# One matmul of 65 columns for two of 33 in a linear attention kernel, with new orders on every engine

## The chip, the core and the metric

The kernel runs on one NeuronCore of a Trainium2 chip. Five engines work side by side and meet at semaphores only: TensorE (PE in the views), VectorE (DVE), ScalarE (ACT), GpSimd (POOL) and SyncE (SP), which here issues DMAs. Each takes its instructions in the order in which the program gives them. The metric is the device time of one execution in microseconds, lower is better.

## The reference, cut to what matters

```
x = x + 0.5 * ffn_block(layernorm(x))
x = x + linear_attention(layernorm(x), Wq, Wk, Wv, Wo, bo)
x = x + 0.5 * ffn_block(layernorm(x))

# linear_attention, B=2, L=4096, E=512, 16 heads of 32
phi_q = elu(q) + 1 ;  phi_k = elu(k) + 1
S = S + phi_k[:, None] * v[None, :]         # running 32x32 state of each head
z = z + phi_k
out = (phi_q @ S) / (sum(phi_q * z) + eps)
```

The feed-forward block chooses `cap = s_len // n_head` tokens for each of its 16 heads; with 2 as the first size of x that is 0, so nothing is added and each block is a normalisation with `ln_g` and `ln_b`. These stages are the first and the last of the kernel.

## The kernel before

The 4096 positions are cut into 32 chunks of 128, and both batch elements (b = 0, 1) are worked in each. Inside a chunk the attention is done densely: scores of 128 x 128 per head, masked causally, times the values, plus the product of the queries with the state left by the earlier chunks. To keep fp32 accuracy with fp16 operands every number is held as a high and a low fp16 half, and a product is made of three matmuls: high with high, high with low, low with high (`PASSES`).

One pass of the loop works on four chunks at once, each at another stage: the newest is loaded and normalised (`front_...`), the next is projected to k, q and v (`project_k`, `project_q`, `project_v`), the next goes through attention (`scores`, `attend`, `update`, `project_out`), and the oldest is normalised a last time and stored (`back_...`, `store_y`). `ops(st)` gives the pieces of one pass. The function `body` of each engine writes the order of its pieces out by hand; `opening` and `closing` do so for the first and last chunks. Between them `body` runs 29 times. Nothing else sets an order: a piece waits by semaphores for its inputs and for the buffers that it overwrites, and all that stands behind it on its engine waits with it.

The attention of one chunk on the engines:

- TensorE, `scores(b, hg)`: 4 heads into one PSUM bank, `SC`. VectorE masks half of them (`mask`), ScalarE copies the other half (`copy_scores`) and GpSimd masks those (`cut`). ScalarE makes the high half of the masked scores `A` (`split_a`), GpSimd the low half.
- TensorE, `attend(b, hf)`: 8 heads, 4 matmuls each: `QS` with the state `SS` (L1640), then the three of `PASSES`, `A` with `VN` (L1643). All have 33 columns: 32 values and a column for the denominator (`DA`). The sums lie in the two banks of `AV`.
- ScalarE, `sums(b)` (L776) copies the 16 denominators to `DEN`. VectorE inverts them (`reciprocals`, L1205) and `quotient(b)` (L1216) multiplies `AV` by them into `TP`. ScalarE and VectorE split `TP` into halves of `ATTN` (`attn_half`, L784, `attn_low`, L1235). SyncE turns it by a DMA (`turn_attn`), and `project_out(b)` (L1675) reads the result `AT`.
- TensorE, `update(b, hf)` (L1661) writes this chunk's share of the state into `AV`, once `quotient` has read it. VectorE adds it to `S` (`add_s`, L1228), and `attend` of the other b may then overwrite `AV`.

The projections share the banks `PJ`: `project_q(b)`, `project_v(b)`, `project_out(b)`, `project_k(b)` follow each other in `PJ[b]`. So `project_v(b)` waits for `low_q(b)` (L1174), the last reader of q, and `project_out(b)` for `low_v(b)` (L1195), the last reader of v. `project_k(b)` waits for the turned `XT` (`turn_x`), `scores(b, 0)` for the turned `KS` and `QS` (`turn_k`, `turn_q`). `front_stats` and `back_gain` (L1273), `back_y` (L1282) are pieces of the first and the last stage on VectorE.

Of the kernel before, what the change touches and what calls it, by code (L numbers as in the profile page):

```python
# [8 lines left out]
P = 128  # L9
BATCH, LEN, E = 2, 4096, 512  # L10
# [3 lines left out]
C = 128  # L14
# [30 lines left out]
WIDTH = H // 2 * DA  # L45

# [15 lines left out]
def build(nc, x, Wq, Wk, Wv, Wo, attn_bo, ln_g, ln_b, out):  # L62
    with ExitStack() as ctx:
# [9 lines left out]
        def sig(name, per, by=1, base=0):  # L73
# [14 lines left out]
        sumsq = sb("sumsq", [P, 4, GROUPS])  # L88
# [34 lines left out]
        VN = [sb(f"VN{p}", [P, BATCH, 2, H, DA], F16) for p in range(2)]  # L123
# [17 lines left out]
        wsq = Y[:, 0]  # L141
# [5 lines left out]
        AV2 = ps("AV", (P, 2, E))  # L147

# [49 lines left out]
                                                     sig("rden_done", 2), sig("attn_done", 2))  # L198
        st_filled = sig("st_filled", 4)
# [66 lines left out]
        def _(sp):  # L266
# [79 lines left out]
            def opening():  # L346
                early, first, second = ops(Step(0, -2)), ops(Step(0, -1)), ops(Step(0, 0))
                early.turn_x(0)
                early.turn_x(1)
                first.turn_k(0)  # L350
                first.turn_k(1)
                first.turn_q(0)
                first.turn_x(0)
                first.turn_x(1)
                first.turn_q(1)
                second.turn_k(0)
# [4 lines left out]
            def closing():  # L361
                fourth, third, second = ops(Step(0, steps - 3)), ops(Step(0, steps - 2)), ops(Step(0, steps - 1))
                fourth.turn_q(0)
                fourth.turn_attn(0)
                fourth.turn_attn(1)
                fourth.turn_x(0)
                fourth.turn_x(1)
                fourth.turn_q(1)
# [12 lines left out]
            sp.wait_ge(y_stored.sem, y_stored.at(steps - 1, 1))  # L381
# [3 lines left out]
        def _(pool):  # L385
# [131 lines left out]
            def body(st):  # L517
# [5 lines left out]
                prev.split_a(1, 3)  # L523
                prev.spread_q(1)
                prev.rstd1_of_x1()
                now.cut(0, 1)
                prev.spread_k(1)
                now.rstd0_of_x()
                now.split_a(0, 0)
                now.split_a(0, 1)  # L530
                now.split_a(0, 2)
                now.x1_bias()
                now.cut(0, 3)
                now.rstd2_of_x2()
                prev.split_s(0)
                now.split_a(0, 3)
                now.cut(1, 1)
                now.split_a(1, 0)
                now.spread_k(0)
                prev.split_s(1)  # L540

            def opening():
# [6 lines left out]
                first.spread_k(1)  # L549
                first.rstd1_of_x1()  # L550
                first.spread_q(0)
                first.spread_q(1)
                second.x1_bias()
# [5 lines left out]
                second.split_a(0, 2)  # L559
                second.split_a(0, 3)  # L560
                second.cut(1, 1)
# [6 lines left out]
            def closing():  # L568
                fourth, third, second, last = ops(Step(0, steps - 3)), ops(Step(0, steps - 2)), ops(Step(0, steps - 1)), ops(Step(0, steps))
                fourth.cut(1, 3)  # L570
                fourth.spread_q(0)
                fourth.split_a(1, 1)
                fourth.split_a(1, 2)
                fourth.split_a(1, 3)
                fourth.rstd1_of_x1()
                fourth.spread_k(1)
                third.cut(0, 1)
                third.split_a(0, 0)
                fourth.spread_q(1)
                third.cut(0, 3)  # L580
                fourth.split_s(0)
                fourth.split_s(1)
                third.rstd2_of_x2()
                third.split_a(0, 1)
                third.split_a(0, 2)
                third.split_a(0, 3)
                third.spread_k(0)
                third.spread_k(1)
                third.spread_q(0)
                third.cut(1, 1)  # L590
                third.split_a(1, 0)
                third.split_a(1, 1)
                third.cut(1, 3)
                third.spread_q(1)
                third.split_a(1, 2)
                third.split_a(1, 3)
                second.split_a(0, 0)
                second.split_a(0, 2)
                third.split_s(0)
                third.split_s(1)  # L600
                third.x1_bias()
                second.rstd2_of_x2()
                second.split_a(1, 0)
                second.split_a(1, 2)
# [7 lines left out]
        def _(act):  # L612
            a = nc.scalar


            def square(j, c):

                m = W_ORDER[j]
                act.wait_ge(w_loaded[m], 16)
                if j or c:  # L620
                    act.wait_ge(w_summed, j * GROUPS + c)
                a.activation(wsq, wnat[m][:, c], ACT.Square, accum_out=sumsq[:, m, c:c + 1]).then_inc(w_summed, 1)  # L622
# [8 lines left out]
            def ops(st):  # L631
# [3 lines left out]
                class Ops:  # L635
# [8 lines left out]
                    def store_y():  # L644
# [4 lines left out]
                        a.dma_start(out[:, bass.ds(back * C, C), :].rearrange("b p e -> p b e"), Y[:]).then_inc(y_stored.sem, 16)  # L649

# [108 lines left out]
                    def v_half(b):  # L759
# [6 lines left out]
                        a.activation(VN[st.parity(1)][:, b, HI, :, 0:D], PJ[b].rearrange("p (h d) -> p h d", h=H),  # L766
                                     ACT.Copy, scale=V_SCALE).then_inc(v_hi.sem, 1)

                    def sums(b):
# [5 lines left out]
                        av = AV2[:, :, 0:2 * QUADS * DA].rearrange("p f (h d) -> p f h d", d=DA)  # L775
                        a.activation(DEN[:, b], av[:, :, :, D], ACT.Identity, bias=den_eps[:, 0:1]).then_inc(den_done.sem, 1)  # L776
# [19 lines left out]
            def body(st):  # L796
                now, prev = ops(st), ops(st.before())
                prev.copy_scores(1, 3)
                prev.back_scale(1)
                prev.sums(0)  # L800
                prev.q_half(0)
# [1036 lines left out]
```

## Time and profile before

| what | value |
|---|---|
| median of 3 runs | 933.3 us (933.2 to 936.84) |
| the profiled execution | 931.69 us |
| its span, first to last instruction | 929.8 us |
| TensorE busy | 900.6 us, 97% |
| VectorE busy | 832.3 us, 90% |
| ScalarE busy | 756.8 us, 81% |
| GpSimd busy | 705.3 us, 76% |
| mean granted TensorE clock | 0.996 |

The profiled execution's time holds 1.89 us outside its span, and lies 1.6 us under the median. Busy times are unions of the engines' own instructions. A view in order of time gives for each row its start, the duration, and in square brackets how long the engine had been idle before it and what released it. The duration of a matmul reaches past the start of the next one, since they are pipelined: the distance between starts is what a matmul costs, and the same holds, to a smaller degree, for the other engines.

### The profile page before, as it was taken

Reading aid. Unit: us, or ns where it says so; the run is one execution under the profiler, and the core shown is the slowest. Engines: PE = TensorE matmul, PEld = TensorE weight load, DVE = VectorE, ACT = ScalarE, POOL = GpSimd, SP = SyncE. Lnnn points to the kernel's source line nnn. Section 1 sums busy time; section 2 is a strip of 40 time slices with the busy share of each in tenths; the row PEclk is TensorE's granted clock in tenths of the full one; section 3 lists DMA queues with packets and bytes.
Section 4 is the critical chain, followed back from the end, with each engine's and each line's share of the span. In section 5 each row is a group of like instructions: output and inputs, shape, how many; then the busy total and the mean of one; then the engine's idle time right before and its main releaser. Section 6 shows DMA issues by size and latency. Waiting matters only on the chain.

```text
span 929.8 us, 30016 instructions
## 1 busy us (share of the span) xinstructions
PE 900.6 (97%) x10278; PEld 527.0 (57%) x10278; DVE 832.3 (90%) x1539; ACT 756.8 (81%) x1323; POOL 705.3 (76%) x869
## 2 busy tenths in 40 slices
PE   4999999999999999999999999999999999999995
PEld 3455555655555665555565655556555556555562
DVE  6989898999999999999999999999999999988885
ACT  6988888888888888888888888888888888888752
POOL 1469777779777778877778977777887777897661
PEclk9999999999999999999999999999999999999999
DMA  8576698876677767668767667776766876766873
GB/s 292 94 152 133 141 179 160 150 138 151 147 162 159 162 138 150 151 143 180 158 146 143 148 147 160 159 165 137 154 147 144 176 158 150 142 129 125 155 121 69
DMA packets 421421, 139.82 MB, mean 150 GB/s; under 512 B 402560, under 2 KB 402560, under 8 KB 421376
## 3 DMA queue, kind: packets, MB, share of 16 engines
q1 hardware_dynamic: 404496, 106.73, 61.6%
q10 hardware_dynamic: 16880, 32.51, 10.6%
q8 instruction: 26, 0.43, 0.2%
q14 instruction: 19, 0.16, 0.1%
HBM read 21.76 MB, written 16.78 MB: 41 GB/s over the span
## 4 chain that ended last, share of the span: by engine, by line
PE 85%; DVE 5%; DMA 4%; ACT 2%; issue 2%; POOL 1%; SPq 0%; ACTq 0%; POOLq 0%; DVEq 0%
PE PJ L1564 48%; PE PJ L1675 17%; PE AV L1643 8%; PE SC L1616 6%; PE AV L1661 5%; PE AV L1640 2%; DMA AT<-ATTN 2%; DMA A<-in_L_attn_Wk_dram 1%; DMA KS<-KN 1%; ACT Y L622 1%; DVE TP L1273 1%; DVE AM L1151 1%; DVE wT L1065 0%; DVE Y L1282 0%; ACT QN L722 0%
## 5 line engine op out<-in xcount | busy, mean ns | idle before, releaser
L1564 PE MATMUL PJ<-wT,XT 128*128 128x512 f16 x2304 | 524.8, 380 | 1.4 <-DMA XT<-XH 0.6
L1564 PEld LDWEIGHTS PJ<-wT,XT 128*128 128x128 f16 x2304 | 216.9, 98 | 245.4 <-issue 3.9
L490 POOL TENSOR_TENSOR A<-AM,A 128x512 f16<-128x512 f32 x252 | 288.2, 1164 | 32.1 <-ACT A L757 32.1
L1675 PE MATMUL PJ<-wT,AT 128*128 128x512 f16 x768 | 176.1, 379 | 2.7 <-DMA AT<-ATTN 2.6
L480 POOL TENSOR_SCALAR_AFFINE_SELECT AM<-AM 128x512 f32<-128x512 f32 x124 | 79.6, 642 | 113.1 <-ACT AM L744 113.1
L757 ACT ACTIVATE A<-AM 128x512 f16<-128x512 f32 x256 | 154.0, 631 | 12.3 <-POOL AM L480 8.9
L1675 PEld LDWEIGHTS PJ<-wT,AT 128*128 128x128 f16 x768 | 71.1, 97 | 80.1 <-DMA AT<-ATTN 4.1
L1643 PE MATMUL AV<-VN,A 128*128 128x33 f16 x3072 | 116.2, 178 | 0.0
L1640 PE MATMUL AV<-SS,QS 128*128 128x33 f16 x1024 | 111.6, 178 | 1.2 <-DVE TP L1216 1.2
L1643 PEld LDWEIGHTS AV<-VN,A 128*128 128x128 f16 x3072 | 108.8, 96 | 3.5
L1151 DVE TENSOR_TENSOR AM<-SC,causal 128x512 f32<-128x512 f32 x132 | 89.7, 682 | 18.2 <-PE SC L1616 18.2
L1640 PEld LDWEIGHTS AV<-SS,QS 128*128 128x128 f16 x1024 | 98.1, 96 | 5.3 <-POOL A L490 1.7
L744 ACT ACTIVATE AM<-SC 128x512 f32<-128x512 f32 x124 | 74.4, 600 | 23.5 <-PE SC L1616 23.4
L1616 PEld LDWEIGHTS SC<-QS,KS 96*128 96x128 f16 x1024 | 68.1, 97 | 32.2 <-issue 0.9
L1616 PE MATMUL SC<-QS,KS 96*128 96x128 f16 x1024 | 83.7, 219 | 1.5 <-DVE AM L1151 0.6
L702 ACT ACTIVATE PHI<-PJ,inv_scale 128x512 f32<-128x512 f32 x64 | 43.6, 682 | 41.9 <-PE PJ L1564 41.9
L513 POOL TENSOR_TENSOR SS<-S,SC_HI 128x528 f16<-128x528 f32 x62 | 73.7, 1189 | 3.3 <-ACT SC_HI L792 3.3
L423 POOL TENSOR_TENSOR X1BO<-X,obias 128x1024 f32<-128x1024 f32 x32 | 75.5, 2360 | 0.2 <-DVE X L1246 0.2
L498 POOL COPY KN<-KN 128x1024 f16<-128x1024 f16 x64 | 66.4, 1037 | 8.4 <-ACT KN L732 8.4
L722 ACT ACTIVATE QN<-PJ,f_scale 128x1024 f16<-128x1024 f32 x64 | 72.0, 1127 | 0.2
L1111 DVE SCALAR_TENSOR_TENSOR X<-TP,stat,shift 128x512 f32<-128x512 f32 x64 | 47.7, 747 | 19.4 <-POOL X1BO L423 19.2
L776 ACT ACTIVATE DEN<-AV,den_eps 128x16 f32<-128x16 f32 x64 | 17.9, 279 | 57.5 <-PE AV L1643 57.5
(106 smaller groups left out, 1574.9 us busy)
## 6 DMA issues: line engine op xcount, KB each, us to landing
out_dram<-Y ACTq DMA_DIRECT2D x31, 512.0 KB, 3.2
X<-in_L_attn_x_dram ACTq DMA_DIRECT2D x30, 512.0 KB, 3.5
X<-in_L_attn_x_dram SPq DMA_DIRECT2D x2, 512.0 KB, 8.0
A<-in_L_attn_Wk_dram SPq DMA_DIRECT2D x1, 1024.0 KB, 8.0
A<-in_L_attn_Wq_dram SPq DMA_DIRECT2D x1, 1024.0 KB, 10.2
QS<-in_L_attn_Wv_dram SPq DMA_DIRECT2D x1, 1024.0 KB, 12.4
QS<-in_L_attn_Wo_dram SPq DMA_DIRECT2D x1, 1024.0 KB, 15.9
XT<-XH SPq DMA_TRANSPOSE x64, 3.5
```

The costliest lines, as they stand in the source:

```text
L423: g.tensor_tensor(X1BO[:, st.parity(1)], X1[:], obias[:].unsqueeze(1).to_broadcast([P, BATCH, E]), ALU.add).then_inc(x1bo_done.sem, 1)
L480: g.affine_select(out=am, in_=am, compare_op=ALU.is_ge, fill=0.0, base=0, pattern=[[0, QUADS], [1, C]], channel_multiplier=-1).then_inc(sc ...
L490: g.tensor_tensor(A[:, b, LO, hg], AM[:, k % 4], A[:, b, HI, hg], ALU.subtract).then_inc(a_lo.sem, 1)
L513: g.tensor_tensor(SS[:, b], S[:, b], SC_HI[:, b], ALU.subtract).then_inc(s_lo.sem, 1)
L744: a.activation(AM[:, k % 4], SC[hg % 2][:], ACT.Copy, scale=SUM_DOWN).then_inc(sc_copied.sem, 1)
L757: a.activation(A[:, b, HI, hg], AM[:, k % 4], ACT.Copy).then_inc(a_hi.sem, 1)
L1151: v.tensor_tensor(AM[:, k % 4].rearrange("p (h q) -> p h q", h=QUADS), SC[hg % 2][:].rearrange("p (h q) -> p h q", h=QUADS), causal[:].uns ...
L1564: ins = t_.matmul(PJ[b], XT[:, w, c, b * C:(b + 1) * C], wT[m_][:, m, c, :], start=(c, w, m) == todo[0], stop=(c, w, m) == todo[-1])
L1616: ins = t_.matmul(SC[hg % 2][:, h * C:(h + 1) * C], KS[cur][0:STACK, head, b * C:(b + 1) * C], QS[cur][0:STACK, head, b * C:(b + 1) * C], ...
L1640: t_.matmul(to, QS[cur][:, head, b * C:(b + 1) * C], SS[:, b, hf, j * DA:(j + 1) * DA], start=True, stop=False)
L1643: ins = t_.matmul(to, A[:, b, w, hg, h * C:(h + 1) * C], VN[cur][:, b, m, head, :], start=False, stop=(w, m) == PASSES[-1])
L1675: ins = t_.matmul(PJ[b], AT[:, b, w, c * C:(c + 1) * C], wT[3][:, m, c, :], start=(c, w, m) == todo[0], stop=(c, w, m) == todo[-1])
```

## The change

In `attend`, the high half of `A` meets high and low values in one matmul: `VN` now holds for each head 32 high values, the denominator's column and 32 low values side by side (`DV` = 65 columns). The product of `A` high with the low values therefore lands beside the rest, in columns of its own. It has to be added later: ScalarE copies these columns of `AV` to `VL` (`spare_sums`), and VectorE adds them to the others into `TP` (`join_sums`). The 8th head of a bank has no room for 65 columns (7 x 65 + 33 = 488 of 512), so it is done as before, and `VL` is zero there. `quotient` then multiplies `TP` in place. `update` waits for `join_sums` instead of `quotient`, and `DEN`. Its matmuls of low values have 32 columns instead of 33.

All orders written out by hand are new. In the opening the four squares of each weight matrix are one instruction, an Exp on one column stands ahead of all else on ScalarE, and TensorE takes the norms of the third matrix ahead of the first projection. In the closing the last tile is scaled, finished and stored in two halves of 256 columns. A bound in the scale of q and k goes from 64 to 32, which changes values and no instruction.

```diff
+DV = DA + D
+WIDE = H // 2 - 1
-        VN = [sb(f"VN{p}", [P, BATCH, 2, H, DA], F16) for p in range(2)]
+        VN = [sb(f"VN{p}", [P, BATCH, H, DV], F16) for p in range(2)]
+        VL = sb("VL", [P, 2, H // 2, D])
+        def heads_of_av(first, last, to):
+            return bass.AP(AV2, first, [[2 * E, P], [E, 2], [DV, to], [1, last - first]])
...
+                    def spare_sums(b):
+                        act.wait_ge(*av_filled.upto(s, 2 * b + 1))
...
+                        a.activation(VL[:, :, 0:WIDE], heads_of_av(DA, DV, WIDE), ACT.Copy).then_inc(low_copied.sem, 1)
...
+                    def join_sums(b):
+                        dve.wait_ge(*low_copied.upto(s, b))
+                        dve.wait_ge(*den_done.upto(s, b))
...
+                        v.tensor_tensor(TP[b][:].rearrange("p (f h d) -> p f h d", f=2, d=D), heads_of_av(0, D, H // 2),
+                                        VL[:], ALU.add).then_inc(av_summed.sem, 1)
...
-                            t_.matmul(to, QS[cur][:, head, b * C:(b + 1) * C], SS[:, b, hf, j * DA:(j + 1) * DA],
-                                      start=True, stop=False)
-                            for w, m in PASSES:
-                                ins = t_.matmul(to, A[:, b, w, hg, h * C:(h + 1) * C], VN[cur][:, b, m, head, :],
-                                                start=False, stop=(w, m) == PASSES[-1])
+                            if j < WIDE:
+                                t_.matmul(AV2[:, hf, j * DV:(j + 1) * DV], a_high, vn, start=True, stop=False)
+                            else:
+                                t_.matmul(to, a_high, vn[:, 0:DA], start=True, stop=False)
+                                t_.matmul(AV2[:, hf, j * DV:j * DV + D], a_high, vn[:, DA:DV], start=False, stop=False)
+                            t_.matmul(to, a_low, vn[:, 0:DA], start=False, stop=False)
+                            ins = t_.matmul(to, QS[cur][:, head, b * C:(b + 1) * C], SS[:, b, hf, j * DA:(j + 1) * DA],
+                                            start=False, stop=True)
...
                     def update(b, hf):
-                        pe.wait_ge(*attn_done.upto(s, b))
+                        pe.wait_ge(*av_summed.upto(s, b))
+                        pe.wait_ge(*den_done.upto(s, b))
...
             # TensorE, body
-                prev.project_v(1)
                 now.scores(0, 0)
                 now.scores(0, 1)
+                prev.project_v(1)
+                now.scores(0, 2)
+                prev.update(1, 0)
+                now.scores(0, 3)
                 prev.project_out(0)
-                now.scores(0, 2)
-                now.scores(0, 3)
-                prev.update(1, 0)
                 prev.update(1, 1)
```

VectorE, in the loop, from `add_s(0)` to `attn_low(1)`, before (names with their buffer numbers; `S<-AV` is `add_s`, `QN<-PJ` `low_q`, `TP<-AV,RDEN` `quotient`):

```order
L1228 SCALAR_TENSOR_TENSOR S<-AV,S 128x528
L1235 SCALAR_TENSOR_TENSOR ATTN<-TP0,ATTN 128x512
L1273 SCALAR_TENSOR_TENSOR TP1<-X2,stat2,TP1 128x512
L1174 SCALAR_TENSOR_TENSOR QN<-PJ,f_scale,QN 128x16x32
L1282 SCALAR_TENSOR_TENSOR Y<-TP1,stat2,shift 128x512
L1205 RECIPROCAL RDEN<-DEN 128x16
L1216 TENSOR_TENSOR TP1<-AV,RDEN 128x512
L1195 SCALAR_TENSOR_TENSOR VN0<-PJ,VN0 128x16x32
L1235 SCALAR_TENSOR_TENSOR ATTN<-TP1,ATTN 128x512
```

and now, with `TP1<-AV,VL` being `join_sums(1)`:

```order
L1267 SCALAR_TENSOR_TENSOR S<-AV,S 128x528
L1110 BN_STATS raw<-X 128x6
L1197 SCALAR_TENSOR_TENSOR PJ<-PHI,PJ 128x512
L1312 SCALAR_TENSOR_TENSOR TP1<-X2,stat2,TP1 128x512
L1274 SCALAR_TENSOR_TENSOR ATTN<-TP0,ATTN 128x512
L1334 SCALAR_TENSOR_TENSOR Y<-TP1,stat2,shift 128x512
L1204 SCALAR_TENSOR_TENSOR QN<-PJ,f_scale,QN 128x16x32
L1235 RECIPROCAL RDEN<-DEN 128x16
L1246 TENSOR_TENSOR TP1<-AV,VL 128x512
L1255 TENSOR_TENSOR TP1<-TP1,RDEN 128x512
L1181 TENSOR_TENSOR AM<-SC0,causal 128x512
L1274 SCALAR_TENSOR_TENSOR ATTN<-TP1,ATTN 128x512
```

`low_q(1)` was the 4th from `add_s(0)` and is the 7th; `low_v(0)` stood ahead of `attn_low(1)` and comes behind it.

TensorE, in the loop, from the last heads of `attend(1, 1)`, before:

```order
L1640 MATMUL AV<-SS,QS 128x33
L1643 MATMUL AV<-VN,A 128x33 x3
L1564 MATMUL PJ<-wT,XT 128x512 x12
L1616 MATMUL SC<-QS,KS 128x128 x8
L1675 MATMUL PJ<-wT,AT 128x512 x12
L1616 MATMUL SC<-QS,KS 128x128 x8
L1661 MATMUL AV<-VN,KN 128x33 x32
```

and now (the 8 heads of `update(1, 0)` follow the last row shown, 2 matmuls each):

```order
L1708 MATMUL AV<-VN,A 128x33
L1709 MATMUL AV<-VN,A 128x32
L1710 MATMUL AV<-VN,A 128x33
L1711 MATMUL AV<-SS,QS 128x33
L1678 MATMUL SC<-QS,KS 128x128 x8
L1626 MATMUL PJ<-wT,XT 128x512 x12
L1678 MATMUL SC<-QS,KS 128x128 x4
L1730 MATMUL AV<-VN,KN 128x33
```

The first two `scores` moved ahead of `project_v(1)`, and `update(1, 0)` ahead of `project_out(0)`.

ScalarE, in the loop, from `sums(1)` to `attn_half(1)`, before:

```order
L776 ACTIVATE DEN<-AV,den_eps 128x16
L766 ACTIVATE VN<-PJ 128x16x32
L683 ACTIVATE TP<-X,offset,rstd 128x512
L784 ACTIVATE ATTN<-TP 128x512
L732 ACTIVATE KN<-PHI,f_scale 128x16x32
```

and now:

```order
L755 ACTIVATE KN<-PHI,f_scale 128x16x32
L799 ACTIVATE DEN<-AV,den_eps 128x16
L809 ACTIVATE VL<-AV 128x2x224
L661 DMA out_dram<-Y 128x2x512
L767 ACTIVATE AM<-SC 128x512
L789 ACTIVATE VN<-PJ 128x16x32
L817 ACTIVATE ATTN<-TP 128x512
```

`spare_sums(1)` (`VL<-AV`) stands behind `sums(1)`, and the store of the finished chunk, which stood behind `copy_scores(0, 3)`, behind it.

## Rows read from the trace of the kernel before

**Rows 1.** Busy time by stretch: window, length, each engine (instructions), clock, DMA
```profile
0.00:30.00 30.00, 15.46 (x66) 10.12 (x67) 22.32 (x64) 21.49 (x47) 6.95 (x22) 1.00 0.76 237
30.00:60.00 30.00, 28.26 (x222) 15.99 (x221) 27.40 (x55) 27.80 (x50) 15.97 (x20) 1.00 0.57 123
...
360.00:420.00 60.00, 60.00 (x747) 35.82 (x744) 55.51 (x104) 51.15 (x90) 49.56 (x60) 1.00 0.68 146
...
900.00:929.80 29.80, 18.91 (x205) 9.92 (x202) 18.83 (x33) 7.32 (x13) 8.19 (x10) 0.94 0.25 54
```

**Rows 2.** TensorE in order of time, one chunk: start, duration, line, operation, count
```profile
415.44 0.39 PE L1616 MATMUL SC<-QS,KS 96*128 96x128 f16 x4
...
416.49 2.75 PE L1564 MATMUL PJ<-wT,XT 128*128 128x512 f16 x12
419.08 0.97 PE L1661 MATMUL AV<-VN,KN 128*128 128x33 f16 x32
419.89 2.75 PE L1564 MATMUL PJ<-wT,XT 128*128 128x512 f16 x12
422.48 0.18 PE L1640 MATMUL AV<-SS,QS 128*128 128x33 f16 x1
...
424.11 2.75 PE L1564 MATMUL PJ<-wT,XT 128*128 128x512 f16 x12
426.70 0.61 PE L1616 MATMUL SC<-QS,KS 96*128 96x128 f16 x8
427.14 2.75 PE L1675 MATMUL PJ<-wT,AT 128*128 128x512 f16 x12
...
442.85 0.38 PE L1616 MATMUL SC<-QS,KS 96*128 96x128 f16 x4
```

**Rows 3.** VectorE in order of time, same chunk
```profile
421.24 0.70 DVE L1228 SCALAR_TENSOR_TENSOR S<-AV,S 128x528 f32<-128x528 f32 x1
...
422.45 0.75 DVE L1273 SCALAR_TENSOR_TENSOR TP<-X,stat,TP 128x512 f32<-128x512 f32 x1
423.11 0.75 DVE L1174 SCALAR_TENSOR_TENSOR QN<-PJ,f_scale,QN 128x512 f16<-128x512 f32 x1
...
424.97 0.70 DVE L1216 TENSOR_TENSOR TP<-AV,RDEN 128x512 f32<-128x512 f32 x1
425.58 0.68 DVE L1195 SCALAR_TENSOR_TENSOR VN<-PJ,VN 128x512 f16<-128x512 f32 x1
426.36 0.69 DVE L1235 SCALAR_TENSOR_TENSOR ATTN<-TP,ATTN 128x512 f16<-128x512 f32 x1
```

**Rows 4.** ScalarE in order of time, same chunk
```profile
424.38 0.27 ACT L776 ACTIVATE DEN<-AV,den_eps 128x16 f32<-128x16 f32 x1 [1.74 <-PE AV L1643]
424.55 0.59 ACT L766 ACTIVATE VN<-PJ 128x512 f16<-128x512 f32 x1
...
425.74 0.59 ACT L784 ACTIVATE ATTN<-TP 128x512 f16<-128x512 f32 x1
...
427.78 0.61 ACT L744 ACTIVATE AM<-SC 128x512 f32<-128x512 f32 x1
```

**Rows 5.** VectorE in the first chunks, two operations that TensorE waits for
```profile
40.02 0.75 DVE L1174 SCALAR_TENSOR_TENSOR QN<-PJ,f_scale,QN 128x512 f16<-128x512 f32 x1 [0.24 <-ACT QN L722]
...
53.06 0.68 DVE L1181 SCALAR_TENSOR_TENSOR PHI<-PHI,PJ 128x512 f32<-128x512 f32 x1
```

**Rows 6.** TensorE in the first chunks, the two matmul groups that waited
```profile
40.91 2.75 PE L1564 MATMUL PJ<-wT,XT 128*128 128x512 f16 x12 [0.36 <-DVE QN L1174]
...
53.80 2.76 PE L1564 MATMUL PJ<-wT,XT 128*128 128x512 f16 x12 [0.15 <-DVE PHI L1181]
```

**Rows 7.** DMA issues of 431 to 433 us: kind, count, us to landing
```profile
XT<-XH SPq DMA_TRANSPOSE x1, 3.6
```

**Rows 8.** DMA issues of 184.1 to 186.1 us, an early chunk
```profile
XT<-XH SPq DMA_TRANSPOSE x1, 4.4
```

**Rows 9.** DMA issues of 427 to 428 us
```profile
AT<-ATTN SPq DMA_TRANSPOSE x1, 3.1
```

More of the change, by code:

```diff
@@ L536, in body @@
                 now.split_a(0, 3)
+                prev.split_s(1)
                 now.cut(1, 1)
+                now.spread_k(0)
                 now.split_a(1, 0)
-                now.spread_k(0)
-                prev.split_s(1)
             def opening():
@@ L548, in opening @@
                 first.spread_k(0)
-                first.spread_k(1)
                 first.rstd1_of_x1()
                 first.spread_q(0)
+                first.spread_k(1)
+                second.x1_bias()
                 first.spread_q(1)
-                second.x1_bias()
                 second.rstd0_of_x()
@@ L973, in closing @@
                 second.split_a(1, 1)
+                second.split_a(1, 2)
                 third.s_half(1)
@@ L976, in closing @@
                 second.back_scale(0)
-                second.split_a(1, 2)
+                second.back_scale(1)
+                second.spare_sums(0)
                 second.split_a(1, 3)
-                second.back_scale(1)
+                second.sums(1)
                 second.attn_half(0)
-                second.sums(1)
+                second.spare_sums(1)
                 second.attn_half(1)
@@ L1297, in body @@
-                prev.phi_q(1)
-                prev.add_s(0)
-                prev.attn_low(0)
-                prev.back_gain(1)
-                prev.low_q(1)
-                prev.back_y(1)
-                prev.reciprocals(1)
-                prev.quotient(1)
-                prev.low_v(0)
-                prev.attn_low(1)
+                prev.phi_q(1)
+                prev.back_gain(1)
+                prev.attn_low(0)
+                prev.back_y(1)
+                prev.low_q(1)
+                prev.reciprocals(1)
@@ L1307, in body @@
+                prev.join_sums(1)
+                prev.quotient(1)
+                now.mask(0, 0)
+                prev.attn_low(1)
+                prev.low_v(0)
+                now.front_stats(1)
+                now.mask(0, 2)
+                prev.x_low(0)
+                prev.low_v(1)
                 prev.low_k(1)
-                now.mask(0, 0)
-                prev.x_low(0)
+                prev.add_out(0)
+                prev.x_low(1)
                 now.front_mean(0)
                 now.front_mean(1)
-                prev.low_v(1)
@@ L1358, in opening @@
                 top_norm(1)
+                scale_w(1)
                 w_low(0, 1)
                 w_low(0, 2)
-                scale_w(1)
                 early.x_low(0)
+                early.x_low(1)
                 w_low(0, 3)
@@ L1521, in closing @@
                 last.back_y(0)
-                last.back_gain(1)
-                last.back_y(1)
+                last.back_gain_part(0)
+                last.back_gain_part(1)
+                last.back_y_part(0)
+                last.back_y_part(1)
             closing()
@@ L1746, in opening @@
                 second.scores(1, 0)
+                second.scores(1, 1)
                 second.project_q(0)
-                second.scores(1, 1)
                 second.scores(1, 2)
@@ L1788, in closing @@
                 second.scores(0, 1)
+                third.attend(1, 0)
                 second.scores(0, 2)
-                third.attend(1, 0)
                 third.attend(1, 1)
@@ L1794, in closing @@
                 second.scores(1, 0)
+                third.update(1, 0)
                 second.scores(1, 1)
-                third.update(1, 0)
                 third.update(1, 1)
+                second.scores(1, 2)
                 third.project_out(0)
                 third.project_out(1)
-                second.scores(1, 2)
                 second.scores(1, 3)
```

445 lines of the change are left out of this document (240 added, 205 removed).

## The prediction

> **What bounds the kernel now.** I read the busy time by stretch first. In the middle TensorE is busy 60.00 of 60 us, VectorE 55.51, ScalarE 51.15, GpSimd 49.56; TensorE is idle only in the first 60 us (14.54 + 1.74) and in the last 30 (10.89) [rows 1]. Then one chunk in order of time: from 415.44 to 442.85 no row of TensorE names a wait, so a chunk costs 27.41 us, all of it matmuls [rows 2]. The loop has 29 chunks, 795 of 929.8 us. VectorE has only some 2.1 us of a chunk left (4.49 of 60).
>
> **What the wide matmul gives.** From 422.48 to 424.11 stand the 64 matmuls of `attend(1, 0)` and `(1, 1)`, so 33 columns cost 25.5 ns. Eight of 128 columns cost 0.44 us (426.70 to 427.14), 55 ns each, and twelve of 512 cost 2.59 (416.49 to 419.08), 216 ns [rows 2]. 65 columns stand in no row. They can't cost less than 33 (25.5), and if they cost twice that (51) nothing is won. The line through 55 and 216 gives 0.419 ns a column and 28.6 ns at 65; I take it, since the larger shapes lie on it and only the smallest sits on a floor. An `attend` of 8 heads then takes 7 x (28.6 + 51) + 4 x 25.5 = 659 ns against 815, so a chunk's four save 0.62 us (0.71 at 25.5, 0 at 51). If TensorE stayed the bound: 0.62 x 32 chunks = 20 us.
>
> The Trainium skill, "TensorE: Matmul & The Clock Gate", Part 1, has start to start as columns over 2.4 GHz plus 2.5 ns, with a floor of some 25 ns. By that 65 columns are 29.6 ns, and a chunk would save 0.59 instead of 0.62. It speaks against the idea that half of the matmul's columns come free, and the rows agree with its floor (25.5).
>
> **What the change adds.** Per chunk VectorE gets two `join_sums`, of the form of `quotient` [rows 3]: 0.70 long, 0.61 from start to start when other work follows, 1.22 a chunk. Its 25.3 become 26.5, and its spare time in a chunk of 26.8 would be 0.3. ScalarE gets two copies of 448 values a partition; 16 values take 0.27, 512 take 0.61 [rows 4], so 0.56 each. ScalarE has 4 us left in a chunk, that is covered unless TensorE waits for it. So the question is who waits at the new places. I laid one chunk of the new order out by hand, each operation at the distances of rows 3 and 4 (0.60 or 0.61 for most on VectorE, 0.66 where `back_gain` stands, 422.45 to 423.11). Handoffs: matmul to ScalarE 0.27 (424.11 [rows 2] to 424.38 [rows 4]); ScalarE to VectorE 0.03 (425.74 + 0.59 to 426.36); VectorE to TensorE 0.14 and 0.06 (40.02 + 0.75 to 40.91; 53.06 + 0.68 to 53.80 [rows 5, 6]), I take 0.10. A dependent operation of VectorE starts some 0.04 after the end of its source, an estimate by the ScalarE handoff.
>
> **First new wait, `project_v(1)` for `low_q(1)`.** TensorE reaches it after `update(0, 1)` in 2.59 (`project_v(0)`) + 1.32 (two `attend`) + 0.44 (two `scores`) = 4.35 us. VectorE can begin `add_s(0)` only when that update is done, and now has seven operations up to `low_q(1)`, where it had four and had started them with others behind: 0.27 + `add_s` 0.61 + `front_stats` 0.60 + `phi_q` 0.61 + `back_gain` 0.66 + `attn_low` 0.60 + `back_y` 0.66 + `low_q` 0.75 + 0.10 = 4.86. `project_v(1)` starts 0.51 late in each chunk. In the kernel before `low_q(1)` ended at 423.86 and `project_v(1)` began at 424.11: it was already close.
>
> **Second new wait, `project_out(0)` for `low_v(0)`.** From the end of `attend(1, 1)` TensorE needs 0.44 + 2.59 + 0.22 + 0.41 + 0.22 = 3.88 us of its own (two `scores`, `project_v(1)`, `scores`, `update`, `scores`). The chain beside it: 0.27, `sums` 0.17 (424.38 to 424.55), `spare_sums` 0.56, 0.03, `join_sums` 0.70 + 0.04, `quotient` 0.70, 0.03, `attn_half` 0.59, 0.03, `attn_low` 0.60, `low_v` 0.68, 0.10: 4.50 [rows 3, 4]. So `project_out(0)` starts 0.62 late in all; the first wait is contained in that. Before, `low_v(0)` stood ahead of `attn_low(1)` and there was no `join_sums`, so it hung on none of this.
>
> A chunk is then 27.41 - 0.62 + 0.62 = 27.41: the matmuls' gain is waited away at the same place in every chunk. Uncertainties: 0.04 either way from the handoff, 0.10 less at 25.5 ns for 65 columns, 0.15 more if ScalarE or VectorE is still at another operation when its turn comes.
>
> **Other moved steps, with one answer.** `update(0, 0)` waits for `join_sums(0)`: the copy is ready about 1.9 us into the chunk, the sum at 2.7, TensorE comes at 3.46 (0.22 + 0.66 + 2.59). Cover 0.7, given by `project_q(1)`. `scores(0, 0)` moved 2.6 us ahead and needs `QS`, of which the DMA lands near 8.2 by my layout, when TensorE arrives; what it waits, up to 0.5, is part of the wait at `project_v(1)`. GpSimd (`split_s`, `x1_bias`, `spread_k` moved) is needed by nobody at once: the layout leaves over 0.6 everywhere.
>
> **DMA.** `project_k(1)` waits for `XT`. Before, `x_low(1)` ended some 4.65 us ahead of it. Now, counted from the start of `low_v(0)`: seven operations on VectorE lead to the end of `x_low(1)` at 5.03, its DMA is issued 0.10 later and lands 3.6 later [rows 7], at 8.73; TensorE arrives at 0.68 + 0.10 + 2.59 + 0.41 + 2.59 + 2.59 = 8.96. The slack shrinks to 0.23. In early chunks (100 to 200 us) the same DMA takes 4.4 [rows 8], which makes it 0.57 late; four such chunks: +2.3. `project_out(1)` for `AT` (3.1 [rows 9]) keeps 0.5.
>
> **Ends.** Opening: merged squares free ScalarE some 1.1 us for each of the first two weights, but TensorE now waits for the third matrix's norm ahead of the first projection. Idle there is 16.28 in all, most of it weights not yet loaded; I take -0.5 (-2.5 to +1.5). Closing: two chunks without a first stage, where VectorE has air, give 2 x -0.62; the last chunk's chain gets longer by the copy and the sum twice (+0.9 on the one that ends last) less its faster matmuls (-0.3), and the halves of the last tile save 0.3: -0.9 (-3 to +2).
>
> **Sum.** 29 chunks x 0.0, +2.3, -0.5, -0.9 = +0.9 on the profiled span of 929.8, 930.7, or 932.6 with the 1.89 around it. That execution lies 1.6 under the median of 933.3, so against the median 934.2.
>
> **Rivals.** (1) *TensorE stays the bound.* If VectorE's operations stand closer than my layout, the waits vanish, a chunk is 26.8, and the time 934.2 - 18 = 916. For it: 2.1 us idle on VectorE against 1.2 added. Against: it needs two chains to shrink by 0.5 and 0.6. Chance 0.14. (2) *Part of the gain.* Some 0.25 to 0.4 of each 0.6 is recovered, as one operation fewer in the way (0.3 on average) would do: 0.3 x 29 = 9, so 925. Chance 0.20. (3) *The DMA decides, slower.* Above 3.83 us for `XT` in the loop TensorE waits at `project_k(1)` too. It is late by 0.37 if the transposes take 4.2 instead of 3.6: 0.37 x 29 = 11, so 945. For it: 4.4 is on record; against: the store of 512 KB moved away from this transpose. Chance 0.17. (4) *The wide matmul costs two narrow ones.* Then 0.62 comes back on the second chain: 934.2 + 18 = 952. Nothing in the rows suggests it; 0.03.
>
> **How the numbers follow.** The forecast, both waits and an unchanged chunk, has 0.46; its own range is 928 to 941 (29 x -0.1 to +0.15, and the ends). The range given reaches from 919, which leaves out rival 1, to 946, which leaves out rival 4 and a tail of rival 3: 0.19 in all. A measurement tells 0.5% (4.7 us) from no change: faster takes rivals 1 and 2 and 0.03 of the forecast, 0.37; slower rivals 3 and 4 and 0.04 of it, 0.24; same 0.39.
>
> **What would show it.** In the middle TensorE should be idle some 0.6 us a chunk, in two waits, at `project_v(1)` for `QN` and at `project_out(0)` for `VN`, and two starts of the same piece 27.4 apart. An `attend` of 8 heads should take 0.66, `spare_sums` 0.56, `join_sums` 0.70. VectorE should be over 96% busy. If TensorE shows 60.00 again, rival 1 is right; if it waits for the DMA of `XT`, rival 3; if 65 columns cost 51 ns, rival 4. The prediction falls if VectorE finds `add_s(0)` ready with work already done ahead, or if its operations stand less than 0.6 apart.

## The result and the profile after

The changed kernel takes 969.1 us (median of 6 runs, 967.0 to 971.8) against 933.5 (6 runs): ratio 1.037, 95% interval 1.036 to 1.039. The forecast was 934.2 with a range of 919 to 946: the time lies outside it, on the side that had a chance of 0.24. The profiled execution has a span of 966.9, 37.1 more than before.

From the page of the changed kernel, the busy time, the chain that ended last, and the group of `project_out` (busy, mean ns | idle before, and what ended it):

```profile
span 966.9 us, 28559 instructions
...
PE 901.4 (93%) x9382; PEld 513.6 (53%) x9382; DVE 870.9 (90%) x1600; ACT 789.6 (82%) x1365; POOL 708.8 (73%) x869
...
PE 48%; SPq 13%; DMA 11%; DVE 8%; issue 4%; ACT 0%; DVEq 0%; POOL 0%; ACTq 0%
...
L1744 PE MATMUL PJ<-wT,AT 128*128 128x512 f16 x768 | 176.3, 379 | 29.2 <-DMA AT<-ATTN 26.4
```

Only 48% of the chain is TensorE (85% before); 13% is SyncE's queue issuing transposes and 11% their flight. `project_out` (L1744) waited 26.4 us for `AT`, a DMA for which it waited 2.6 us before, none of it between 200 and 800 us.

How long is a chunk? The start of `x1_bias` on GpSimd, the same instruction in each chunk, gives it. First before, then after (start, duration):

```profile
187.67 2.37 POOL L423 TENSOR_TENSOR X1BO<-X,obias 128x1024 f32<-128x1024 f32 x1 [0.19 <-DVE X L1246]
...
764.18 2.37 POOL L423 TENSOR_TENSOR X1BO<-X,obias 128x1024 f32<-128x1024 f32 x1
```
```profile
197.37 2.35 POOL L433 TENSOR_TENSOR X1BO<-X,obias 128x1024 f32<-128x1024 f32 x1 [2.38 <-DVE X L1285]
...
766.57 2.35 POOL L433 TENSOR_TENSOR X1BO<-X,obias 128x1024 f32<-128x1024 f32 x1 [1.68 <-DVE X L1285]
```

21 chunks lie between the first two, 20 between the others: 27.45 us a chunk before, 28.46 after. Of the 37.1 us, 9.7 are there by the first of these rows, 21 x 1.01 = 21.2 come in the middle, and 6.2 at the end.

One chunk of the changed kernel on TensorE, in order of time, beside [rows 2]:

```profile
437.49 2.75 PE L1626 MATMUL PJ<-wT,XT 128*128 128x512 f16 x12
440.08 0.19 PE L1706 MATMUL AV<-VN,A 128*128 128x65 f16 x1
...
441.39 0.18 PE L1711 MATMUL AV<-SS,QS 128*128 128x33 f16 x1
441.74 0.62 PE L1678 MATMUL SC<-QS,KS 96*128 96x128 f16 x8 [0.17 <-DMA QS<-QN]
442.22 2.76 PE L1626 MATMUL PJ<-wT,XT 128*128 128x512 f16 x12
...
445.94 2.75 PE L1744 MATMUL PJ<-wT,AT 128*128 128x512 f16 x12
449.79 2.76 PE L1744 MATMUL PJ<-wT,AT 128*128 128x512 f16 x12 [0.70 <-DMA AT<-ATTN]
```

`project_v(0)` starts at 437.49, so `update(0, 1)` ended there; `project_v(1)` starts at 442.22, 4.73 later (the forecast's chain: 4.86), and 0.06 after `low_q(1)` has ended (441.42 + 0.74). TensorE's own work in between is 4.38, so it is 0.35 late, where 0.51 was forecast. The 16 heads of `attend(1, 0)` and `(1, 1)` run from 440.08 to some 441.43; from there to `project_out(0)` at 445.94 are 4.51 us (forecast: 4.50); TensorE's own 3.88 leave 0.63 of waiting in all (forecast: 0.62), in which the first wait is contained. Up to here the chunk runs as predicted. What was not foreseen is the last row: `project_out(1)` starts 3.85 after `project_out(0)`, where an update (0.41) and twelve matmuls (2.59) need 3.00. That is 0.85 us of waiting for `AT`. Over 200 to 800 us the view of waits gives 17.4 us in 21 such waits, 0.83 each where this one has 0.70, so the mean loss is 0.13 larger: 0.98 a chunk.

What SyncE's queue and ScalarE's queue issued in this stretch, first before, then after (start and duration of the issue):

```profile
422.63 1.23 SPq L330 DMA_TRANSPOSE AT<-ATTN  x1
424.25 1.67 SPq L319 DMA_TRANSPOSE QS<-QN  x1
427.15 1.23 SPq L330 DMA_TRANSPOSE AT<-ATTN  x1
429.02 3.92 SPq L291 DMA_TRANSPOSE XT<-XH  x2
...
430.77 0.40 ACTq L649 DMA_DIRECT2D out_dram<-Y  x1
```
```profile
440.94 1.24 SPq L340 DMA_TRANSPOSE AT<-ATTN  x1
442.57 3.74 SPq L329 DMA_TRANSPOSE QS<-QN  x1
446.62 1.23 SPq L340 DMA_TRANSPOSE AT<-ATTN  x1
448.14 3.28 SPq L301 DMA_TRANSPOSE XT<-XH  x2
...
441.91 0.40 ACTq L661 DMA_DIRECT2D out_dram<-Y  x1
```

The store of 512 KB, which stood behind `AT(1)` before, now goes out 0.7 us ahead of `QS(1)`. The issue of `QS(1)` takes 3.74 us instead of 1.67 and holds the queue until 446.31. `attn_low(1)` had been done since 445.20 (444.51 + 0.69), but `AT(1)` is issued at 446.62, behind `QS(1)` in the same queue. The DMA views of both stretches agree: `QS(1)` lands after 5.6 us instead of 4.3, while `AT(1)`, once issued, takes 3.1 as before. What `AT(1)` lost is its start.

**Theory A**: the store lengthens the transpose that it overlaps, which delays the next one in the queue, and TensorE waits for whichever has the least slack. **Rival B**: `QS(1)` is slow because it follows `AT(0)` closely, or something else in the order is at fault; or the added work of VectorE sets the chunk anyway.

### The profile page after: what moved, and what is told of

The parts are those of the page before. It is cut to its first block, busy times and chain, and to the rows that moved or that the text cites. A ratio compares the mean times of both kernels' runs of the same rounds, so it can differ in the third digit from the quotient of the medians.

```text
span 966.9 us, 28559 instructions
## 1 busy us (share of the span) xinstructions
PE 901.4 (93%) x9382; PEld 513.6 (53%) x9382; DVE 870.9 (90%) x1600; ACT 789.6 (82%) x1365; POOL 708.8 (73%) x869
## 3 DMA queue, kind: packets, MB, share of 16 engines
q10 hardware_dynamic: 17024, 32.51, 10.1%
## 4 chain that ended last, share of the span: by engine, by line
PE 48%; SPq 13%; DMA 11%; DVE 8%; issue 4%; ACT 0%; DVEq 0%; POOL 0%; ACTq 0%
PE PJ L1626 30%; SPq L329 9%; DMA AT<-ATTN 9%; PE PJ L1744 9%; SPq L340 3%; PE SC L1678 3%; DVE TP L1312 2%; DVE raw L1110 2%; DVE ATTN L1274 2%; PE AV L1706 2%; PE AV L1711 1%; PE AV L1731 1%; PE AV L1730 1%; DVE PJ L1197 1%; PE AV L1710 1%
## 5 line engine op out<-in xcount | busy, mean ns | idle before, releaser
L1744 PE MATMUL PJ<-wT,AT 128*128 128x512 f16 x768 | 176.3, 379 | 29.2 <-DMA AT<-ATTN 26.4
L1744 PEld LDWEIGHTS PJ<-wT,AT 128*128 128x128 f16 x768 | 70.4, 97 | 112.5 <-DMA AT<-ATTN 30.3
L1678 PE MATMUL SC<-QS,KS 96*128 96x128 f16 x1024 | 88.9, 219 | 10.4 <-issue 6.3
L1710 PE MATMUL AV<-VN,A 128*128 128x33 f16 x1024 | 94.5, 178 | 0.0
L1711 PE MATMUL AV<-SS,QS 128*128 128x33 f16 x1024 | 94.4, 177 | 0.0
L1706 PE MATMUL AV<-VN,A 128*128 128x65 f16 x896 | 86.4, 191 | 1.9 <-DVE TP L1246 1.9
L1710 PEld LDWEIGHTS AV<-VN,A 128*128 128x128 f16 x1024 | 86.1, 96 | 3.7
L1285 DVE SCALAR_TENSOR_TENSOR X<-PJ,out_scale,X1BO 128x512 f32<-128x512 f32 x64 | 47.9, 748 | 43.7 <-PE PJ L1744 43.4
L1711 PEld LDWEIGHTS AV<-SS,QS 128*128 128x128 f16 x1024 | 85.9, 96 | 0.0
L1678 PEld LDWEIGHTS SC<-QS,KS 96*128 96x128 f16 x1024 | 65.9, 97 | 35.9 <-issue 12.1
L1706 PEld LDWEIGHTS AV<-VN,A 128*128 128x128 f16 x896 | 75.3, 96 | 6.1 <-issue 2.3
```

The lines of the kernel that those rows point to most:

```text
L1678: ins = t_.matmul(SC[hg % 2][:, h * C:(h + 1) * C], KS[cur][0:STACK, head, b * C:(b + 1) * C], QS[cur][0:STACK, head, b * C:(b + 1) * C], ...
L1706: t_.matmul(AV2[:, hf, j * DV:(j + 1) * DV], a_high, vn, start=True, stop=False)
L1710: t_.matmul(to, a_low, vn[:, 0:DA], start=False, stop=False)
L1711: ins = t_.matmul(to, QS[cur][:, head, b * C:(b + 1) * C], SS[:, b, hf, j * DA:(j + 1) * DA], start=False, stop=True)
L1744: ins = t_.matmul(PJ[b], AT[:, b, w, c * C:(c + 1) * C], wT[3][:, m, c, :], start=(c, w, m) == todo[0], stop=(c, w, m) == todo[-1])
```

## Experiments: where the store stands

**The store back behind a later step, and an early store in the kernel before.**

```diff
# changed kernel, ScalarE
-                prev.store_y()
                 now.copy_scores(0, 1)
...
                 now.copy_scores(0, 3)
+                prev.store_y()
```

> The changed kernel with one line moved: in the loop ScalarE issues the store of the finished chunk behind copy_scores(0, 3), about where the kernel before had it, instead of behind spare_sums(1). Theory A (the store of 512 KB runs beside the transpose of QS for b = 1, whose issue then holds SyncE for 3.74 us instead of 1.7 to 2.0, so turn_attn(1) comes 1.3 us late and project_out(1) waits 0.88 us): the issue of QS for b = 1 takes under 2.2 us, project_out(1) no longer waits for AT, a chunk goes from 28.35 to 27.5 us, 29 chunks give 25 us, time 944 (940 to 949). Rival B (the issue is slow since it follows the transpose of ATTN by 0.39 us, or because three transposes are in flight): nothing changes, 967 to 971.

Measured: 982.0 us (ratio 1.053, 1.051 to 1.055), worse still, where theory A had 944. The issue of `QS(1)` is down to 1.79, and the wait for `AT` is gone. But now the store goes out 0.7 us behind `XT(0)`, and the wait has moved:

```profile
444.79 1.79 SPq L329 DMA_TRANSPOSE QS<-QN  x1
447.53 1.23 SPq L340 DMA_TRANSPOSE AT<-ATTN  x1
...
450.60 0.40 ACTq L661 DMA_DIRECT2D out_dram<-Y  x1
```
The waits of TensorE in this kernel, 200 to 800 us (total, times, longest), and two lines on the transposes of `XT` there:
```profile
PE PJ L1626 <- DMA XT<-XH: 22.4, 20, 1.2
...
L301 SPq DMA_TRANSPOSE XT<-XH x42: 1232/1260/1297, 219.9 to 797.6; - x42
...
DMA to landing us min/median/max: 3.5/4.4/5.1
```

`XT` lands after 3.5 / 4.4 / 5.1 us (shortest, median, longest) against 3.0 / 3.1 / 3.3 in the changed kernel. By the DMA view of this chunk it is `XT(0)`, in whose issue the store falls, that takes 5.1, and `XT(1)`, issued 1.8 us after the store, 3.7. So what was expected of `QS(1)` and `AT(1)` came true, and the total did not, because the store met another transpose for which TensorE has no slack of 2 us.

```diff
# kernel before, ScalarE
                 prev.sums(1)
+                prev.store_y()
...
-                prev.store_y()
```

> The kernel before with one line moved: the store stands behind sums(1) on ScalarE, some 6 us earlier, at about 424.6 in its trace, 0.4 us behind the issue of QS for b = 1 (424.25). Theory A: the issue of QS for b = 1 or the transpose behind it gets longer; up to 2 us more there makes turn_attn(1) up to 1.3 late against a slack of 0.75, so a chunk costs 0 to 0.5 us more: 933 to 948, and the landing of QS for b = 1 is over 5 us. Rival B: 933 unchanged, landing 4.3.

Measured: 958.5 us (1.027, 1.024 to 1.029): the store alone, put early, costs the kernel before 25 us, more than the 15 that I allowed. A chunk takes 28.08 (13 us over the 21 chunks), and 12 us are lost ahead of them. `QS` lands after 4.3 / 5.2 / 6.6 us (before 4.2 / 4.3 / 4.6) and `AT` after up to 3.9 (before 3.3). TensorE's matmuls wait for `AT` 8.3 us in 21 chunks (200 to 800), 0.4 us each. ScalarE, which here must wait for `back_y(1)` in front of the store, loses 0.7 a chunk ahead of its next operation (15.1 us in 21), so this run supports A without isolating it.

**The queue's order.**

```diff
# changed kernel, SyncE
                 prev.turn_attn(0)
+                prev.turn_attn(1)
                 prev.turn_q(1)
-                prev.turn_attn(1)
```

> The changed kernel with one exchange on SyncE in the loop: turn_attn(1) ahead of turn_q(1), the store left where the change put it. Theory A: AT for b = 1 is issued when attn_low(1) ends and lands before project_out(1), that wait (0.88 us) goes; the transpose of QS is issued some 3 us later, behind the store's 3.7 us, takes 2 us to issue and makes turn_x(0) 1.4 late, of which 0.7 reaches project_k(0): a chunk about 28.1, time 962 (955 to 968). Rival B (slow whenever it follows another transpose closely): the issue stays at 3.7, turn_x(0) comes 3 us late and a chunk takes 30 us or more, over 1000.

Measured: 978.1 us (1.050, 1.047 to 1.053), where theory A had 962. `QS(1)`, which SyncE now issues once `attn_low(1)` is done and the store is over, takes 2.17 us in one chunk and 2.04 in the next, though it follows a transpose of `AT` by 0.32 and 0.38 us (0.39 in the changed kernel): that speaks against B. The wait moves to `XT` again (20.7 us in 21 chunks), since everything in the queue is later.

**The store thinned.**

```diff
# changed kernel, loop only
-  a.dma_start(out[:, bass.ds(back * C, C), :].rearrange("b p e -> p b e"), Y[:])
+  a.dma_start(out[:, bass.ds(back * C, C), 0:16].rearrange("b p e -> p b e"), Y[:, :, 0:16])
```

> The changed kernel, but in the loop the store of a finished chunk writes 16 of each row's 512 columns; the other 496 columns of the output of the loop's chunks are left out. Its issue stays where it was, only 496/512 of its bytes go. Theory A (the 512 KB of the store lengthen the transposes that it overlaps, QS(1) above all, and AT(1) is issued late behind it): the issue of QS(1) on SyncE falls from 3.74 to at most 2.2 us, project_out(1) no longer waits for AT (0.87 us a chunk), XT(0) and XT(1) land in 3.1 us; chunk 27.5 us instead of 28.35, total 942 to 947. Rival B (QS(1) is slow for another reason, such as following AT(0) closely, or VectorE's added work decides the chunk): 964 to 970.

The kernel leaves out 496 of the 512 columns of the output in the loop's chunks.

Measured: 942.0 us (1.010, 1.008 to 1.011). This is the decisive run: orders, waits and instructions are those of the changed kernel, only the bytes of one DMA are missing, and 27 of the 36 us are gone. The store is issued 0.7 us ahead of `QS(1)` as before, and the queue reads

```profile
427.57 0.40 ACTq L661 DMA_DIRECT2D out_dram<-Y  x1
...
428.24 1.97 SPq L329 DMA_TRANSPOSE QS<-QN  x1
430.97 1.23 SPq L340 DMA_TRANSPOSE AT<-ATTN  x1
```

**The whole store, where no transpose is issued.**

```diff
# changed kernel, ScalarE
-                prev.store_y()
                 now.copy_scores(0, 1)
...
                 now.exp_relu_k(0)
+                prev.store_y()
```

> The changed kernel with nothing left out; in the loop ScalarE issues the store of a finished chunk behind exp_relu_k(0), some 23 us into the chunk, where no transpose is in flight. Theory A (the store costs by the transposes that it overlaps): no wait for AT and none over 0.3 us for XT, the issue of QS(1) at most 2.2 us, chunk 27.5 us, total 940 to 950. Rival B (VectorE or the order of the two first waits decides): 964 to 970. Rival C (the store now lengthens KS and the load of X, and the features of the keys come late): 955 to 975.

Measured: 941.6 us (1.011, 1.008 to 1.015), with nothing left out. The issue of `KS(1)` is over at 440.71 (438.93 + 1.78), 1.0 us ahead of the store at 441.69, and the next one begins at 448.84:

```profile
429.73 1.67 SPq L329 DMA_TRANSPOSE QS<-QN  x1
432.46 1.23 SPq L340 DMA_TRANSPOSE AT<-ATTN  x1
434.85 3.74 SPq L301 DMA_TRANSPOSE XT<-XH  x2
...
438.93 1.78 SPq L314 DMA_TRANSPOSE KS<-KN  x1
...
441.69 0.40 ACTq L661 DMA_DIRECT2D out_dram<-Y  x1
```
My words "where no transpose is in flight" were not exact: `KS(1)` lands only 4.4 us after its issue, at 443.3, so the store meets its last 1.6 us. Neither suffers (`KS` 4.3 / 4.4 / 4.5 us in 44, the store 2.8). The slack that the prediction gave to `AT` is there too: `AT(1)` lands at 435.56 (432.46 + 3.1), and `project_out(1)` starts at 436.10, 0.54 later. The waits of TensorE, 200 to 800 us, and the same two rows of `x1_bias`:
```profile
PE SC L1678 <- DMA QS<-QN: 0.4, 2, 0.2
PE SC L1678 <- issue: 0.2, 1, 0.2
```
```profile
192.50 2.35 POOL L433 TENSOR_TENSOR X1BO<-X,obias 128x1024 f32<-128x1024 f32 x1 [1.96 <-DVE X L1285]
...
769.28 2.36 POOL L433 TENSOR_TENSOR X1BO<-X,obias 128x1024 f32<-128x1024 f32 x1 [0.66 <-DVE X L1285]
```

A chunk is 576.78 / 21 = 27.47 us, against 27.45 before: what the prediction said (27.41, unchanged). Against the changed kernel, this one gains 4.9 us up to the first row, 20.9 in the middle (21 x 0.99) and 1.2 behind: 27.0 us of the 37.1 belong to the place of the store. The other 10.1 are 0.3 in the middle, 4.8 ahead of it and 5.0 behind it.

## Experiments: matmuls, additions, orders

**The new arithmetic in the old order of the loop, with and without the additions.**

```diff
# e4: loop orders of the kernel before, and
                 prev.sums(b)
+                prev.spare_sums(b)
...
+                prev.join_sums(b)
                 prev.reciprocals(b)
# e9: as e4, but spare_sums and join_sums do nothing (in the loop and at both ends), update
# waits for quotient again as in the kernel before, and quotient reads the high sums
-                        v.tensor_tensor(tp, tp,
+                        v.tensor_tensor(tp, heads_of_av(0, D, H // 2),
```

> The new arithmetic in the old order: every engine's loop in the order of the kernel before, with spare_sums put behind sums and join_sums ahead of reciprocals; opening and closing as changed. Theory (the order cost the time, the arithmetic saves 0.54 us of matmuls a chunk but adds 1.22 to a VectorE that has 2.1 left): low_q(1) comes about 0.8 us late for project_v(1), turn_attn(1) in time; a chunk 27.5 to 27.8, time 942 (935 to 948), well below the changed kernel. Rival (the added copy and sum are themselves what costs): 965 or more.

Measured: 965.7 us (1.035, 1.033 to 1.037); my 942 was wrong, the rival's 965 right. A chunk is 28.43. TensorE waits for `low_q` (10.0 us in 42) and `phi_k` (7.9 in 20) between 200 and 800, and VectorE itself waits for GpSimd (14.8 us before):

```profile
DVE X L1141 <- POOL X1BO L433: 26.8, 21, 1.3
```

> The order of before with the wide matmuls of the change, but the low products are neither copied nor added in the loop: the product of A's high half with the low half of V is left out of the result there, for 14 of 16 heads. It measures the matmul side alone. Theory A (the wide matmuls give 0.54 us a chunk, and all that the change loses comes from the copies, the additions and the order made for them): chunk 27.41 - 0.54 = 26.87 us, total 914 to 920. Rival B (TensorE gains nothing that reaches the end, because VectorE or DMA holds the chunk at 27.4): 930 to 935. Rival C (the wide matmuls themselves cost more than the two that they replace): above 936.

e9 leaves out of the result the product of `A`'s high half with the low values for 14 of 16 heads.

Measured: 931.9 us (0.999, 0.998 to 1.000), where theory A had 914 to 920. The busy time of the same stretch (TensorE, weight loads, VectorE first), of before, of e7_store_mid and of this one:

```profile
200.00:480.00 280.00, 280.00 (x3302) 164.44 (x3299) 257.20 (x471) 234.20 (x408) 227.13 (x278) 1.00 0.72 153
```
```profile
200.00:480.00 280.00, 277.79 (x3022) 159.19 (x3017) 268.40 (x492) 246.53 (x430) 228.32 (x276) 1.00 0.71 152
```
```profile
200.00:480.00 280.00, 279.51 (x3034) 161.32 (x3031) 259.15 (x475) 237.97 (x414) 227.24 (x279) 1.00 0.74 156
```
and two starts of `x1_bias` here, 21 chunks apart:
```profile
188.15 2.35 POOL L433 TENSOR_TENSOR X1BO<-X,obias 128x1024 f32<-128x1024 f32 x1 [1.34 <-DVE X L1290]
...
758.24 2.35 POOL L433 TENSOR_TENSOR X1BO<-X,obias 128x1024 f32<-128x1024 f32 x1
```

A chunk is 27.15: the wide matmuls alone give 0.30 us, not the 0.56 that their spacing promises. Part of the rest is a wait of weight loads of the projections for `phi_k`, 0.2 us in two of three chunks (2.3 us in 14 between 200 and 800); the remainder I could not place. In the same order the copies and additions then cost 28.43 - 27.15 = 1.28 us a chunk. With the order of the change and the store out of the way they cost 0.32 (27.47 - 27.15).

**Three attempts to beat both kernels.**

> The store behind exp_relu_k(0) as above, and another order of the chunk's work on ScalarE, VectorE and TensorE: low_q(1) right behind back_gain(1), low_v(0) ahead of attn_low(1), project_v(1) ahead of scores(0,0), the updates ahead of project_out(0). Theory A (with the store out of the way, what is left of the loss is the two waits of 0.64 us for low_q(1) and low_v(0), and an order can hide them): chunk 27.0 to 27.3 us, total 924 to 934. Rival B (VectorE's 1.22 us more leave no order that hides it): chunk 27.8 to 28.4, 950 to 968.

Measured: 957.6 us (1.028, 1.025 to 1.031), in the rival's range; a chunk is 28.11. TensorE waits for `AT` 15.6 us in 21 chunks although no store is near: `attn_low(1)` stands behind `low_v(0)` and both updates ahead of `project_out(0)`, and `project_out(1)` comes before its `AT`. A short slack for `AT` is thus enough for a loss, with or without the store.

```diff
# e7_store_mid, VectorE
+                prev.low_q(1)
                 prev.back_y(1)
-                prev.low_q(1)
...
-                now.mask(0, 0)
-                prev.attn_low(1)
                 prev.low_v(0)
+                prev.attn_low(1)
+                now.mask(0, 0)
```

> e7_store_mid (941.6 us, chunk 27.46) with two moves on VectorE in the loop: low_q(1) ahead of back_y(1), and low_v(0) ahead of attn_low(1), with mask(0,0) behind both. Theory A (with the store out of the way, what is left in the chunk is the wait of project_v(1) for low_q(1), 0.3 us, and of project_out(0) for low_v(0), 0.3 us): chunk 26.9 to 27.2, total 926 to 934. Rival B (VectorE is then the bound: 26.85 us busy in a chunk of 27.46, and the mask that is put back comes late to ScalarE and GpSimd): chunk 27.3 to 27.8, total 937 to 952.

Measured: 964.6 us (1.035, 1.032 to 1.037), above both ranges. The one operation put back, the mask, is waited for at once by the next scores:

```profile
442.28 0.40 PE L1678 MATMUL SC<-QS,KS 96*128 96x128 f16 x4 [1.08 <-DVE AM L1181]
```

The two waits of 0.3 are bought with one of over a microsecond (23.6 us in 21), 28.34 us a chunk. Neither of these two orders of VectorE found a free place between the end of `attend(1, 1)` and `project_out(1)`; that there is none is not shown.

**The ends.** Opening, then opening and closing, in the order of the kernel before, with e7_store_mid's loop:

> The changed kernel with its store behind exp_relu_k(0) as in e7_store_mid (941.6 us), and the opening of all five engines in the order of the kernel before. Theory A (of the 8 us that e7_store_mid still stands above before, some 3 lie in the opening's new order, as the first five chunks, 3.1 us longer than before's, suggest): 937 to 940. Rival B (the opening's loss comes from the added copies and sums in its first chunks, whatever the order): 941 to 943.

Measured: 944.6 us (1.011, 1.009 to 1.013), above both ranges.

> e7_store_mid with the opening and the closing of all engines in the order of the kernel before, the added copies and sums put where their data come. Theory A (the ends of the changed kernel, 3.1 us in the first five chunks and 3.4 in the last two, are losses of their new order): 934 to 938. Rival B (the additions cost that there in any order): 941 to 944.

Measured: 945.2 us (1.012, 1.008 to 1.016). No gain: the old orders don't bring back the 9.8 us at the two ends.

> The two moves of e11_low_first and the ends of e12_old_ends together. If both theories hold: 920 to 930. If neither does: 941 to 955.

Measured: 967.6 us (1.036, 1.033 to 1.040), the loss of e11_low_first again.

No variant is clearly faster than the kernel before; the nearest one that computes everything is e7_store_mid, 1.1% above it.

## Why the prediction was wrong, point by point

- **The wide matmul.** From the first start (440.08) to the last of the 50 (441.39) are 49 steps, 14 of them of 65 columns; less 35 of 25.5 ns they take 0.418 us, 29.8 ns each, where I took 28.6. 16 heads take 1.35 us (440.08 to 441.43) against 1.63 and those of the other batch element 0.68 and 0.67, so a chunk saves 2 x 0.28 = 0.56, not 0.62. The Trainium skill, "TensorE: Matmul & The Clock Gate", Part 1, gives 29.6 by its rule, and the trace agrees with it better than with my line. Rival 4 (51 ns) is out.
- **The two waits of 0.51 and 0.62.** The second was right: 4.51 for 4.50. The first chain was 4.73 for 4.86, and its wait 0.35. `spare_sums` took 0.54 (0.56), `join_sums` 0.70 (0.70). With the store moved away the chunk is 27.47, which is 27.41 - 0.56 + 0.63 = 27.48: the mechanism "the gain is waited away at the same place" held.
- **The step that failed: "`project_out(1)` for `AT` (3.1 [rows 9]) keeps 0.5".** It took the flight of `AT` as before, which was right (3.1), and its issue as following `attn_low(1)` at once, which was not: SyncE's queue issues in order, `QS(1)` stands ahead of `AT(1)`, and the change moves the store beside `QS(1)`. I had counted the store only where it left (rival 3: "moved away from this transpose"), not where it arrived. Its price: `QS(1)` holds the queue 2.07 us longer (3.74 for 1.67), `AT(1)` is issued 1.4 us after `attn_low(1)` has ended, and 0.5 of slack becomes 0.98 of waiting on average. Sum by the measured terms: 27.41 - 0.56 + 0.63 + 0.98 = 28.46, and 28.46 was measured.
- **`XT` and `project_k(1)`, rival 3.** The transposes of `XT` got shorter (median 3.1, before 3.3) as that argument said, and between 200 and 800 us TensorE did not wait for them. Slower by a DMA was the right kind of rival, with the wrong DMA. The 3.6 of [rows 7] was itself a flight beside the store: it was issued 0.86 us behind it (431.63, 430.77), and the transpose ahead of it took 3.0. So the rows of before held a sign that a store lengthens a transpose.
- **The ends, -0.5 and -0.9, and +2.3 for early chunks.** Wrong too: with the store out of the way they are +4.8 and +5.0. In e7_store_mid TensorE waits between 60 and 200 us for `AT` 2.1, for `QS` 1.9 and for the issue of scores 2.4, where before it waited 0.5 in all; behind 845 us for `AT` 3.6 (before 2.0) and for issue 2.9 (before 0.5). Ahead of the middle the added operations are what costs: without them (e9) the first of the two rows of `x1_bias` comes 0.5 later than before, with them in the same order (e4) 7.3 (194.97 for 187.67). Behind it they are not the whole cause, since e9, with no addition anywhere, also takes 5.5 us more than before from its second row to its end, and e12, with the old order of the closing, 5.0. The mean granted clock of the last 30 us was 0.81 in e9, 0.89 in e7_store_mid and 0.94 before, so a part of both may be the clock's. What costs the 5 us at the end stays open.
- **VectorE over 96% busy.** It was busy 260.18 of 280 us (93%), since it waits too while TensorE waits for `AT`; with the store moved away 268.40 (96%).

## What to carry to other kernels

When a change moves a DMA, list which transfers are issued beside its new place, and follow the in-order queue behind that: here a 512 KB store cost nothing to its own engine and 27 us through the transpose beside it. A gain on the bound engine that is paid with work on an engine already some 92% busy should be measured first without the payment (here it was 0.30 us a chunk, and the payment 0.32 in the better order and 1.28 in the other). A forecast of unchanged time that rests on slacks of 0.2 to 0.5 us needs each of those slacks checked against a transfer that is 1 to 2 us longer.

## What the runs showed of the hardware

A DMA transpose from SyncE can be slowed by one plain 512 KB store from another engine's queue, if the two are issued close together. The cases, by the time from the store's issue to the transpose's:

| kernel, transpose | issued after the store by | landing, us | undisturbed |
|---|---|---|---|
| changed, `QS(1)` | 0.66 (442.57 - 441.91) | 5.6, issue 3.74 | 4.3 to 4.5, issue 1.67 |
| before, `XT(1)` | 0.86 (431.63 - 430.77) | 3.6 | 3.0 |
| e1, `XT(1)` | 1.82 | 3.7 | 3.1 |
| e2, `QS(1)` | -0.50 (441.31 - 441.81) | 6.2, issue 1.94 | 4.3 |
| e1, `XT(0)` | -0.69 (449.91 - 450.60) | 5.1 | 3.1 |
| changed, `AT(0)` | -0.97, its issue over 0.27 behind the store's start | 3.1 | 3.1 |
| before, `XT(0)` | -1.75, its issue over by 0.52 (429.02 + 1.23 to 430.77) | 3.0 | 3.0 |
| e7, `KS(1)` | -2.76, its issue over by 0.98 | 4.4 | 4.4 |

A transpose whose issue had ended or nearly ended kept its time, though it was still in flight; one issued between 0.7 us ahead of the store and 0.7 behind it paid 1.1 to 2.0 us, and one issued 0.9 to 1.8 us behind it 0.6. The rows are of three kinds of transpose, so the bounds are rough. The issue that held SyncE's queue for 3.74 us was seen only where `QS` was issued just behind the store; in e2, where it was issued ahead, the flight grew and the issue did not (1.94). The Trainium skill, "DMA: Bandwidth & Descriptors", "Issuing engines are not separate DMA queues", says that DMAs of the scalar, sync and gpsimd engines run on the same 16 DMA engines and interleave. The first five rows agree with it. The store suffers too: 3.7 us in the changed kernel, 4.2 in e1, 4.8 in e2, 2.8 in e7.
